# Second attention of a fused token pipeline: scores over three PSUM banks, half exponentials, masked queries by GpSimd, output projection a step later

## The reference

```python
qk = (x @ Wqk.T).reshape(Bb, Nn, 2, Hh, hd)
q = qk[:, :, 0].transpose(0, 2, 1, 3)
k = qk[:, :, 1].transpose(0, 2, 1, 3)
patch_score = jax.nn.softmax(jnp.einsum('bhnd,bhmd->bhnm', q, k) * scale, axis=-1)
...
attn = (1.0 - g) * patch_score + g * pos_score[None]
attn = attn / attn.sum(axis=-1, keepdims=True)
v = (x @ Wv.T).reshape(Bb, Nn, Hh, hd).transpose(0, 2, 1, 3)
out = jnp.einsum('bhnm,bhmd->bhnd', attn, v)
out = out.transpose(0, 2, 1, 3).reshape(Bb, Nn, Cc)
return out @ Wproj.T + bproj
```

## Time and profile before

| | |
|---|---|
| median of three runs | 621.32 us |
| profiled execution: time, span | 620.74 us, 619.0 us |
| PE busy | 545.0 us (88%) |
| DVE busy | 427.1 us (69%) |
| ACT busy | 358.0 us (58%) |
| POOL busy | 347.0 us (56%) |
| granted PE clock, mean over the span | 0.984 |

### The profile page before, as it was taken

The page is one execution under the profiler, slowest core; times in us unless marked ns, Lnnn a source line. Parts: engine busy times, 40 slices in busy tenths (PEclk is TensorE's granted clock), DMA queues, the critical chain, the costliest instruction groups (busy, mean ns, idle before and its releaser), DMA issues.

```text
span 619.0 us, 12438 instructions
## 1 busy us (share of the span) xinstructions
PE 545.0 (88%) x4494; PEld 414.5 (67%) x4494; DVE 427.1 (69%) x1088; ACT 358.0 (58%) x949; POOL 347.0 (56%) x474
## 2 busy tenths in 40 slices
PE   7989999999987867779788888998999698889996
PEld 3556767778434656558677777886578576765785
DVE  4943563423887868798989988899526987756444
ACT  1264444444676765224768878874696666757430
POOL 2597653311360767798889899998267310001445
PEclk9999999999999999987999999999999999989999
DMA  8000000000000434300000000000000000000000
GB/s 278 17 1 1 2 0 1 1 1 1 1 2 1 75 71 77 81 0 2 2 1 1 1 2 2 0 2 1 2 2 2 1 2 1 2 2 1 9 9 18
DMA packets 10860, 10.43 MB, mean 17 GB/s; under 512 B 6000, under 2 KB 9840, under 8 KB 10544
## 3 DMA queue, kind: packets, MB, share of 16 engines
q1 hardware_dynamic: 8080, 7.54, 4.5%
q0 software_dynamic: 2144, 1.75, 1.5%
q10 hardware_dynamic: 576, 0.35, 0.2%
HBM read 5.77 MB, written 0.52 MB: 10 GB/s over the span
## 4 chain that ended last, share of the span: by engine, by line
PE 52%; DVE 21%; POOL 9%; ACT 7%; issue 5%; DMA 4%; SPq 2%; DVEq 0%; POOLq 0%; ACTq 0%
PE bank L1354 8%; PE bank L1342 7%; PE bank L1441 7%; PE bank L1657 5%; PE bank L1723 5%; DVE bank L2173 3%; PE bank L1615 3%; DVE features L2167 2%; DMA coefs<-weights 2%; PE bank L1720 2%; PE bank L1432 2%; POOL features L600 2%; PE bank L1768 2%; DVE features L2143 2%; SPq L460 2%
## 5 line engine op out<-in xcount | busy, mean ns | idle before, releaser
L1441 PE MATMUL bank<-ident,features 128*128 128x128 f32 x604 | 79.0, 280 | 10.4 <-DVE features L2143 7.1
L1441 PEld LDWEIGHTS bank<-ident,features 128*128 128x128 f32 x604 | 69.0, 145 | 19.0 <-DVE features L2143 13.8
L909 ACT ACTIVATE G<-bank,cols 128x512 f32<-128x512 f32 x64 | 43.9, 687 | 52.9 <-PE bank L1342 52.9
L600 POOL TENSOR_TENSOR features<-UV,coefs 128x1024 f32<-128x1024 f32 (+3 forms) x36 | 59.8, 1684 | 4.0 <-DVE UV L2130 4.0
L1354 PE MATMUL bank<-weights,G 128*128 128x128 f32 x512 | 59.9, 275 | 0.0
L1342 PE MATMUL bank<-xs,weights 128*128 128x512 f32 x128 | 57.8, 594 | 0.9 <-ACT xs L900 0.9
L1354 PEld LDWEIGHTS bank<-weights,G 128*128 128x128 f32 x512 | 58.5, 192 | 0.0
L2143 DVE TENSOR_TENSOR features<-UV,bank 128x1024 f32<-128x1024 f32 (+3 forms) x68 | 55.6, 861 | 0.7 <-ACT bank L992 0.2
L400 POOL TENSOR_SCALAR rstd<-mv 128x4 f32<-128x4 f32 x8 | 1.6, 195 | 92.7 <-DVE mv L412 92.7
L999 ACT ACTIVATE xs<-UV,coefs 128x32 f32<-128x32 f32 x232 | 50.4, 308 | 0.0
L999 ACT ACTIVATE sx<-UV,coefs 128x32 f32<-128x32 f32 x200 | 43.5, 307 | 0.0
(11 more groups left out here) (362 smaller groups left out, 1348.0 us busy)
## 6 DMA issues: line engine op xcount, KB each, us to landing
weights<-in_w SPq DMA_DIRECT2D x2, 1024.0 KB, 10.2
features<-in_tok SPq DMA_DIRECT2D x1, 768.0 KB, 5.8
weights<-in_ew SPq DMA_DIRECT2D x4, 128.0 KB, 3.1
weights<-in_ew SPq DMA_DIRECT2D x2, 256.0 KB, 2.9
coefs<-G POOLq DMA_DIRECT2D x16, 25.5 KB, 4.7
rows<-in_rows SPq DMA_DIRECT2D x1, 384.0 KB, 6.4
out_h<-H SPq DMA_DIRECT2D x3, 128.0 KB, 2.0
coefs<-G SPq DMA_DIRECT2D x14, 25.5 KB, 5.1
```

Source lines behind the costliest of these rows:

```text
L600: pool.tensor_tensor(out, u, co, ALU.mult).then_inc(s["held_p"], 1)
L909: act.activation(G[:, 4 * (w % 2) + f, :], up_bank(f)[:], ACT.Gelu, bias=col("b1", 4 * i + f)).then_inc(s["tok_gelu"], 1)
L1441: last = mm(out[:, P * k:P * k + P], x[:, P * k:P * k + P], ident[:], is_transpose=True, start=first and k == 0, stop=last_ and k == n - 1 ...
```

## The change

Four edits, all in the second attention (two further edits put counts of `utab_mm` and `mean_mm` onto the semaphores `u_mm` and `router_mm`, with the waits raised by one, and move no instruction).

1. Score groups rotate over banks 2, 3 and 5: half n of all 32 halves goes to bank (2, 3, 5)[n % 3]. A score group now waits for the first subtraction of the step before (`s_sub` 2t-1), not for both.
2. The exponential is made in two instructions of 512 numbers. The transposes are called once for each half, both halves into bank 4, each half behind the copy of the half before. ACT's list becomes exponential 0, copy 0, exponential 1, the chunk's parts, copy 1.
3. For chunks 2 and 3, ACT copies the projected queries once (`take_queries`, into `qraw`), and POOL makes the four masked copies from there (`queries` in POOL's list). Chunks 0 and 1 stay as they were.
4. The output projection of chunks 0 and 1 is called one step later (t = 8 and 12) and writes bank 1; the addition and statistics move to j = 1, and `e_apply` to t = 11 and 14.

```diff
+        def score_bank(n):
+            return bank[(2, 3, 5)[n % 3]]
...
+            def queries(c):
+                pool.wait_ge(s["q_raw"], c - 1)
+                for h in range(NH // 2):
+                    pool.tensor_scalar(qd[c % 2][:, h, :], qraw, m4[:, h:h + 1], None, ALU.mult).then_inc(s["d_qpool"], 1)
+            queries(2)
+            rstd_twice(pool, ch, ("e", 0), CH)
+            queries(3)
...
+            def take_queries(c):
+                act.wait_ge(s["d_q"], c + 1)
+                if c == 3:
+                    act.wait_ge(s["d_qpool"], NH // 2)
+                act.activation(qraw, bank[1][:], ACT.Copy).then_inc(s["q_raw"], 1)
...
-                if t:
-                    take_turned(t - 1)
+                exponential(t, 0)
+                take_turned(t, 0)
+                exponential(t, 1)
                 if t == T - 1:
                     take_attended(NC - 2)
-                act.wait_ge(s["s_sub"], 2 * t + 2)
-                act.activation(sexp[:, t % 2], sexp[:, t % 2], ACT.Exp, scale=float(HD) ** -0.5).then_inc(s["s_exp"], 1)
...
+                take_turned(t, 1)
...
                 if t:
-                    pe.wait_ge(s["s_sub"], 2 * t)
+                    pe.wait_ge(s["s_sub"], 2 * t - 1)
...
+            def turn_scores(t, g):
+                pe.wait_ge(s["s_exp"], 2 * t + g + 1)
+                if t or g:
+                    pe.wait_ge(s["p_ready"], 2 * t + g)
+                for j in range(4):
+                    last = tr(bank[4][:, P * j:P * j + P], sexp[:, t % 2, 4 * g + j, :], ident[:])
...
@@ in project_qk
+                if c >= 3:
+                    pe.wait_ge(s["d_add"], c - 2)
...
@@ in project_out
+                if c < 2:
+                    pe.wait_ge(s["d_vcopy"], c + 3)
+                if c == 1:
+                    pe.wait_ge(s["pos_saved"], 2)
...
                 if t + 1 < T:
                     scores(t + 1)
+                turn_scores(t, 0)
...
-                turn_scores(t)
-                if j == 3 and c:
-                    project_out(c - 1)
+                turn_scores(t, 1)
+                if t == T - 1 or j == 0 and c >= 2:
+                    project_out(NC - 2 if j else c - 2)
...
@@ the loop of DVE
-                if j == 0 and c >= 2:
+                if j == 1 and c >= 2:
                     add_attended(c - 2)
                     e_stats(c - 2)
-                if j == 1 and c >= 2:
-                    e_apply(c - 2)
                 if j == 2 and c:
                     mix(c - 1)
+                if t in (11, 14):
+                    e_apply(c - 2)
```

More of the change, by code:

```diff
@@ L368, in turn_bank, with out_bank @@
             return bank[6 if k == 0 else 2 + c if c < 2 else c % 2]
+        def score_bank(n):
+            return bank[(2, 3, 5)[n % 3]]
+        def out_bank(c):
+            return bank[1 if c < 2 else 0]
         def expert_bank(k, c, e):
@@ L869, in _ @@
             second_norm(NC - 1)
-            for c in range(NC):
+            def queries(c):
[5 more added lines that the diff above has]
+            queries(3)
+            for c in range(1, NC):
                 rstd_twice(pool, ch, ("e", c), CH)
@@ L1217, in save_values_T, with exponential, take_turned @@
                 act.activation(avT[:, p % 2, :], bank[6][:], ACT.Copy).then_inc(s["av_saved"], 1)
[L1219 to L1226, removed]
+            def exponential(t, g):
+                act.wait_ge(s["s_sub"], 2 * t + g + 1)
+                x = sexp[:, t % 2, 4 * g:4 * g + 4, :]
+                act.activation(x, x, ACT.Exp, scale=float(HD) ** -0.5).then_inc(s["s_exp"], 1)
+            def take_turned(t, g):
+                act.wait_ge(s["s_T"], 2 * t + g + 1)
+                if t >= 2:
+                    act.wait_ge(s["av_mm"], t - 1)
+                act.activation(pexp[:, t % 2, 4 * g:4 * g + 4, :].rearrange("p h n -> p (h n)"), bank[4][:],
+                               ACT.Copy).then_inc(s["p_ready"], 1)
             save_sums(2)
@@ L1295, in _ @@
             pe.wait_ge(s["load_tables"], 32)
-            mm(bank[0][0:VOC, 0:DT], embT[:], wupd[:], start=True, stop=True).then_inc(s["utab_mm"], 1)
+            mm(bank[0][0:VOC, 0:DT], embT[:], wupd[:], start=True, stop=True).then_inc(s["u_mm"], 1)
             pe.wait_ge(s["tables_ready"], 1)
@@ L1623, in means @@
                 if c == NC - 1:
-                    last.then_inc(s["mean_mm"], 1)
+                    last.then_inc(s["router_mm"], 1)
             tr = nc.tensor.transpose
@@ L1762, in scores @@
                 if t % CH == 0:
-                    pe.wait_ge(s["d_qd"], NH // 2 * (t // CH + 1))
+                    if t < 2 * CH:
+                        pe.wait_ge(s["d_qd"], NH // 2 * (t // CH + 1))
+                    else:
+                        pe.wait_ge(s["d_qpool"], NH // 2 * (t // CH - 1))
                     pe.wait_ge(s["d_kcopy"], t // CH + 1)
                 if t:
-                    pe.wait_ge(s["s_sub"], 2 * t)
+                    pe.wait_ge(s["s_sub"], 2 * t - 1)
                 for j in range(NH // 2):
-                    low = mm(bank[2][:, P * j:P * j + P], q_[0:D, j, n], k_[0:D, n], start=True, stop=True)
-                    high = mm(bank[3][:, P * j:P * j + P], q_[D:P, j, n], k_[D:P, n], start=True, stop=True)
+                    low = mm(score_bank(2 * t)[:, P * j:P * j + P], q_[0:D, j, n], k_[0:D, n], start=True, stop=True)
+                    high = mm(score_bank(2 * t + 1)[:, P * j:P * j + P], q_[D:P, j, n], k_[D:P, n], start=True, stop=True)
                 low.then_inc(s["s_mm0"], 1)
                 high.then_inc(s["s_mm1"], 1)
[L1773 to L1781, removed]
+            def turn_scores(t, g):
[4 more added lines that the diff above has]
+                    last = tr(bank[4][:, P * j:P * j + P], sexp[:, t % 2, 4 * g + j, :], ident[:])
+                last.then_inc(s["s_T"], 1)
             def values(t):
@@ L1853, in project_out @@
                 pe.wait_ge(s["at_xT"], c + 1)
+                if c < 2:
+                    pe.wait_ge(s["d_vcopy"], c + 3)
+                if c == 1:
+                    pe.wait_ge(s["pos_saved"], 2)
                 for j in range(CH):
-                    last = mm(bank[0][:, D * j:D * j + D], xa[:, 1, P * j:P * j + P], wproj[:], start=True, stop=True)
+                    last = mm(out_bank(c)[:, D * j:D * j + D], xa[:, 1, P * j:P * j + P], wproj[:], start=True, stop=True)
                 last.then_inc(s["proj_mm"], 1)
@@ L1978, in _ @@
             one_hot(1)
-            dve.wait_ge(s["utab_mm"], 1)
+            dve.wait_ge(s["u_mm"], 1)
             dve.wait_ge(s["load_update"], 16)
```

36 lines of the change are left out of this document (21 added, 15 removed).

## The result

The changed kernel takes 629.46 us (median of 4 runs, 626.98 to 631.60), the kernel before beside it 620.78 (4 runs, 618.67 to 621.87). The ratio is 1.0152, 95% interval 1.0116 to 1.0189: slower by 1.5%. The forecast was 621.0 with a range up to 622.9, so it was wrong.

What follows compares the result with a forecast made beforehand. PE, the fullest engine, was taken to bound the loop, its waits on DVE giving way to a PE-ACT loop. Span end -0.3 us from 620.74 gave 620.4; with the median 0.6 above, 621.0, range 618.4 to 622.9.

Steps and rivals of the forecast that it cites:

- One input and a column: I take 0.65, nearer the copy: Price of each POOL masked copy, between a copy's 0.61 and products' 1.04 and 1.27 us; four covered by 3.8 us.
- POOL's masked copies are late: Rival: score groups of steps 8 and 12 wait for POOL from 0.95 us each; 623.3 us at 1.27; chance 0.08.
- half clock from 552.00: PE's clock at 0.50 behind the loop in the trace before, priced at 1.44 us.
- The walk: Prices carried through all 16 loop steps in list order; after the change, the transposes behind the loop start at 553.99.
- control: The same walk for the kernel before, checked against its trace; up to 0.9 us late at full clock.
- light step: Loop step from score group to score group without chunk work: 3.98 us before, 3.66 after, a gain of 0.3.
- The step with the positional part and the projection: Step 12's group in the last chunk, with 0.4 us of wait for ACT's copy: 6.04 us to the next group.
- lead: How much sooner than the control the changed walk reaches steps 4, 8, 12 and loop end: 0.7, 0.6, 1.5, -0.1 us.
- The rotation pays: Rival: handovers 0.05 us shorter, half exponential 0.54, light step 3.4; end 2 to 3 us earlier, 618.5; chance 0.26.
- edits 3 and 4 pay: Chunk 2: ACT copies once, the projection leaves the fullest step; steps sum to 17.8 us against 18.7.
- row 15's chain: Loop's end: the chunk's normalisation, 1.1 us, stands ahead of row 15 on DVE; PE idle 2.0 us before its transposes.
- The clock at the loop's end: PE's clock likelier falls again behind 2.0 us idle; span end +0.1 us if it falls, -1.3 if not; -0.3 taken.

Runs made afterwards that it cites:

- kernel with two operations: The changed kernel with each POOL masked copy made with two operations (times the mask, plus 0.0): 619.20 us, ratio 0.9991 to the kernel before.
- products: The changed kernel with POOL's masked copies as products of two tensors: 620.04 us, ratio 1.001 to the kernel before.
- masks on ACT: The changed kernel with edit 3 taken back, so ACT makes the masked copies of all chunks: 626.62 us, ratio 1.0087 to the kernel before.
- number: The changed kernel with POOL's copies multiplied by the number 1 in place of the mask's column, queries unmasked: 629.58 us, ratio 1.0144 to the kernel before.
- fillers: The changed kernel with two matmuls of 512 columns, results unused, ahead of each PE wait for POOL: 625.48 us, ratio 1.0107 to the kernel before.
- forms: The changed kernel with POOL's eight masked copies made in different forms to price them, one execution; no kernel time given.
- two kernels without halves: The changed kernel with edits 1 and 2 taken back: masks as products of two tensors 622.12 us, masks with two operations 617.98 us.
- two misses: On the changed kernel with masks as products: edits 1 and 2 taken back, 622.12 us; chunk 1's masks on POOL too and e_apply(1) behind row 15, 622.74 us.
- first kernel with chunk 1's masks on POOL: The changed kernel with masks as products, chunk 1's made on POOL too, e_apply(1) behind row 15: 622.74 us, ratio 1.0066 to the kernel before.

## Why the prediction was wrong, point by point

**The step that failed** is one term: "One input and a column: I take 0.65, nearer the copy", with 1.27 as its upper bound. It measured 1.56, outside both bounds, and four copies of 6.2 us then stood against a cover of 3.8. The row of the copy was the wrong neighbour for a form with one operation and the right one for a form with two. The tightest proof is the edit of one line: at 0.69 the same kernel has the loop that was forecast (75.64 for 75.8) and the time that was forecast (no change); at 1.04 no change either; at 1.56 1.5% are lost.

**The rival had the mechanism, not the size.** "POOL's masked copies are late" named the groups of steps 8 and 12 and put the decision at 0.95 each. The prediction gave it 2.3 us at 1.27, and its 623.3 there already lay outside the range, which ended at 622.9. Carried on for eight copies to 1.56, that is about 4.6 us (2.3 and 8 times 0.29), my sum. The trace has twice as much, 9.6 more than the kernel with two operations:

- steps 7 to 8 and 11 to 12, which hold the waits: 6.46 and 6.49 for 4.10 and 4.10, 4.75 us together;
- the steps behind them: 5.92 and 7.08 for 4.72 and 4.71, 3.6 us, at half clock;
- the end of the loop: 1.25 us, clock 0.65 for 1.00.

So a wait of 2.3 us on PE cost 3.6 us the first time and 4.8 the second. The prediction knew the half clock from 552.00, priced it at the loop's end, and didn't ask whether the rival's wait would bring it. Its chance of 0.08 was too small for a price that no row showed.

**GpSimd's price by the page.** The Trainium skill's rule that one input runs "roughly line-rate" (GPSIMD Engine Reference, section Engine selection) and the 0.77 us of its cycle count for 512 elements (the same page, section Elementwise — side-by-side cycle accounting) missed by a factor of two: 1.56 measured. The form with two operations, 0.69, and the copy, 0.61, lie near that count.

**The walk held, its control less so.** Starts of steps 4, 8 and 12 after the first group: walk 16.17, 34.16, 51.95; kernel with two operations 16.18, 34.31, 52.03. The first three steps of chunk 1 are 4.17, 5.25, 4.61 (4.15, 5.23, 4.56); a light step (1 to 2) is 3.68 where 3.66 was forecast and 3.98 stood before. The step with the positional part and the projection (13 to 14) was said to take 6.04 and takes 6.22 in both kernels. The control of the kernel before was 75.74 for the loop, where 75.05 is measured at full clock (the prediction took off 1.44 for the half clock, where the same 16 matmuls show 1.20). So the forecast "lead" of -0.1 us is 0.6 us of loss in the traces, and that the time came out unchanged with masks at 0.69 owes something to luck: both differences are under what the times can tell.

**Edits 1 and 2:** the mechanism was right. DVE is out of PE's loop and ACT is in it; half exponentials take 0.63 (0.60 assumed), the waits for them are 0.2 to 0.65, with one of 1.0 and one of 1.5. The groups of ACT in the loop of the changed kernel (count, busy us, mean ns, idle time before):

```profile
L1248 ACT ACTIVATE features<-features 128x512 f32<-128x512 f32 x32 | 20.1, 627 | 1.1 <-DVE features L2542 1.1
L1255 ACT ACTIVATE UV<-bank 128x512 f32<-128x512 f32 x32 | 19.2, 599 | 23.2 <-PE bank L1815 22.8
```

The split gains nothing: without it and with edits 3 and 4 the loop is 74.06, with it 75.64, both at a clock of 1.00; 1.05 of the 1.58 stand behind the last score group (8.09 against 9.14). The rival *The rotation pays* was wrong: its half exponential of 0.54 measured 0.63.

**Edit 4:** a step later costs 0.7 of the loop (75.64 against 74.92, both at a clock of 1.00; the walk said 0.9). In chunk 2 it gains 0.1 (there "edits 3 and 4 pay", as the prediction said); from step 12 to step 15, where the projection shares a step with the positional part, it loses 0.5, and behind the last score group 0.3, by row 15's chain. Row 15's chain in the changed kernel (DVE's timeline, then PE's):

```profile
552.64 1.11 DVE L433 TENSOR_SCALAR xs<-H,mv,rstd 128x128 f32<-128x128 f32 x4
553.67 0.68 DVE L2538 TENSOR_REDUCE RK<-bank 128x4 f32<-128x512 f32 x1
...
555.87 0.66 PE L1815 MATMUL bank<-ident,features 128*128 128x128 f32 x4 [1.50 <-ACT features L1248]
```

PE is idle for 1.50 ahead of row 15's transposes (2.0 forecast). **The clock at the loop's end** was forecast to stay at half. It did in the changed kernel (0.65), and not in the kernel with two operations (1.00), with the same idle of 1.50. Over all traces with this end of the loop and this idle it fell in five (the change, products, masks on ACT, number, fillers) and stayed in two (forms, two operations); behind the idle of 1.63 of the whole exponential it fell before and stayed in the two kernels without halves; behind 1.2 it stayed in all four. What tells the kernels with the same idle apart isn't settled, and with one trace each it may be the execution and not the kernel. `project_qk(3)` does not wait for DVE's addition, as forecast.

**What no case had:** POOL's work holds DVE's. In the changed kernel it is small (an operation of 0.42 took 0.80 at 506.35, the normalisation at 531.24 took 1.65 for 1.11). In the two misses it made the waits longer, and the clock that fell behind them cost as much again or more.

## What to carry to other kernels

An operation that has not run in that form on that engine has no price, and the nearest rows may bound it from one side only. If a forecast hangs on it, ask how late it may be, and give that rival a chance that fits an open upper end. A wait on PE costs more than its length when the clock falls behind it: here 2.3 us cost about 4. Before two loops are compared, look whether their clocks were the same: here that turned a gain of 0.6 us into a loss. And work moved to GpSimd is not free for VectorE: look at which of VectorE's instructions beside it have all their inputs in SBUF.

## What the runs showed of the hardware

- GpSimd, 512 fp32 numbers in each partition: `tensor_scalar` with one operation 1.56 us (column) or 1.49 (number), with two operations 0.69 (column) or 0.63 (number), copy 0.61, product of two tensors 1.04. The form with more arithmetic is the faster one.
- VectorE beside GpSimd: a normalisation of 64 numbers in SBUF takes 0.31 alone and about 1.0 beside GpSimd's products of 1.04, and ends with them. Instructions with an input in PSUM kept their times beside them (0.42, 0.68, 0.69). The slow `tensor_scalar` held VectorE's sum of two tensors for 0.38 us only, of its own 1.56; by the lock of the Trainium skill's page on SBUF, named above, it would have been held to the end. Why it wasn't, no run here tells.
- TensorE's granted clock fell to 0.50 (the 1.2 GHz level) around or behind each of the five waits of 2.0 us and more in these loops (the change and the kernel with a number twice each, the first kernel with chunk 1's masks on POOL once), and in steady work also behind waits of 1.0 to 1.7 us, but not always: behind the 1.0 of step 4 in one trace of nine, behind 1.71 once of two. The stretches lasted some 3 to 10 us. At full clock a score group's matmuls follow at 0.11 us, at the lower one at 0.21.
